# A four-layer adapter block on one core: another order of work inside the slots of its attention stage

## The reference

```python
x = x + einsum('bsi,boi->bso', x, w0[ids])                     # a whole 512x512 weight per sequence
x = x + attention(x)                                           # 32 query heads, 8 key/value heads, D = 128
x = x + einsum('bnr,bor->bno', einsum('bni,bri->bnr', x, B[ids]), A[ids])      # rank 16
x = x + x @ W.T + b + 2 * ((x @ lora_A[slot]) @ lora_B[slot])                  # rank 16
```

```python
def lora_linear(x, w, a, b, ids):
    return x @ w + einsum('btr,bro->bto', einsum('bti,bir->btr', x, a[ids]), b[ids])
p = softmax(where(causal & mask, q @ k.T / sqrt(D), -max))
out = lora_linear(p @ v, wo, ao, bo, ids)
```

## Time and profile before

| | |
|---|---|
| time, median of 3 runs | 808.75 us (807.19 to 808.94) |
| profiled execution | 807.25 us, its span 805.6 us |
| granted TensorE clock, mean | 0.972 of full |
| busy share of the span | PE 93%, PEld 77%, DVE 67%, ACT 40%, POOL 38% |
| attention stage | TensorE from 203.98 us to about 740 us |

### The profile page before, as it was taken

The page is one execution under the profiler, slowest core; times in us unless marked ns, Lnnn a source line. Parts: engine busy times, 40 slices in busy tenths (PEclk is TensorE's granted clock), DMA queues, the critical chain, the costliest instruction groups (busy, mean ns, idle before and its releaser), DMA issues. The chain is left out here.

```text
span 805.6 us, 13257 instructions
## 1 busy us (share of the span) xinstructions
PE 748.7 (93%) x4132; PEld 622.4 (77%) x4132; DVE 537.8 (67%) x1412; ACT 321.5 (40%) x908; POOL 307.5 (38%) x276
## 2 busy tenths in 40 slices
PE   5799398996799999999999999999999999987898
PEld 4688276885688888888888888888888888875686
DVE  4795366886566776667676677666767666653973
ACT  3663233210543453454354345435435433442540
POOL 3554410444362272273345237227324522510410
PEclk9999789999799999999999999999999999999899
DMA  8977777763042124035024112403402212611402
GB/s 296 307 242 212 253 202 213 268 181 113 1 126 58 46 86 118 1 94 153 0 65 131 52 56 74 117 0 109 139 0 65 65 39 66 106 16 33 102 27 79
DMA packets 75228, 86.84 MB, mean 108 GB/s; under 512 B 26791, under 2 KB 44359, under 8 KB 73975
## 3 DMA queue, kind: packets, MB, share of 16 engines
q1 hardware_dynamic: 73138, 79.83, 34.2%
q0 software_dynamic: 1760, 6.49, 2.6%
q10 hardware_dynamic: 292, 0.07, 0.0%
HBM read 71.40 MB, written 20.73 MB: 114 GB/s over the span
## 5 line engine op out<-in xcount | busy, mean ns | idle before, releaser
L994 POOL TENSOR_TENSOR prob<-prob,rinv 128x512 f32<-128x512 f32 x64 | 66.7, 1042 | 216.7 <-DVE rinv L1080 216.7
L943 ACT ACTIVATE prob<-sm,nmax 128x128 f32<-128x128 f32 x256 | 99.7, 391 | 77.9 <-DVE nmax L1065 77.9
L987 POOL TENSOR_TENSOR qt<-qc,qs 128x512 f32<-128x512 f32 x60 | 77.7, 1295 | 95.3 <-DVE qs L1023 95.3
L1155 PE MATMUL ps_out<-wo_hi,ot_hi 128*128 128x512 f32 x256 | 106.6, 416 | 4.3 <-DVE ot_lo L1042 2.4
L932 ACT ACTIVATE ot_hi<-ps_o 128x512 fp32r<-128x512 f32 x64 | 38.1, 595 | 162.6 <-PE ps_o L1143 162.6
L80 PE MATMUL ps_q<-x1t_hi,blk_hi 128*128 128x512 f32 x240 | 100.8, 420 | 0.0
L1157 PE MATMUL ps_out<-wo_hi,ot_lo 128*128 128x512 f32 x256 | 100.6, 393 | 0.0
L1156 PE MATMUL ps_out<-wo_lo,ot_hi 128*128 128x512 f32 x256 | 99.6, 389 | 0.0
L82 PE MATMUL ps_q<-x1t_hi,blk_lo 128*128 128x512 f32 x240 | 95.9, 400 | 0.0
L81 PE MATMUL ps_q<-x1t_lo,blk_hi 128*128 128x512 f32 x240 | 95.8, 399 | 0.0
L1023 DVE TENSOR_TENSOR qs<-ps_q,sin_t 64x512 f32<-64x512 f32 x120 | 82.7, 689 | 3.7
(11 more groups left out here) (208 smaller groups left out, 1727.4 us busy)
## 6 DMA issues: line engine op xcount, KB each, us to landing
wo_raw<-in_wo SPq DMA_DIRECT2D x8, 1024.0 KB, 5.4
raw_w<-in_wq SPq DMA_DIRECT2D x8, 1024.0 KB, 6.8
w_raw<-in_w SPq DMA_DIRECT2D x7, 1024.0 KB, 6.7
raw_b<-bq_sel SPq DMA_DIRECT2D x56, 128.0 KB, 4.3
raw_b<-bkv_sel SPq DMA_DIRECT2D x16, 256.0 KB, 6.7
v_hi_d<-v_hi SPq DMA_DIRECT2D x16, 256.0 KB, 3.1
v_lo_d<-v_lo SPq DMA_DIRECT2D x16, 256.0 KB, 4.0
k_rot<-kr SPq DMA_DIRECT2D x16, 256.0 KB, 3.2
```

The costliest lines, as they stand in the source:

```text
L943: e = act.activation(prob[i][:, h, :], sm[:, h, :], ACT.Exp, bias=nmax[i][:, h:h + 1], scale=-1.0, accum_out=rsum[i][:, h:h + 1])
L987: pool.tensor_tensor(qt[:, half, h, :], qc[:, :], qs[:, :], ALU.add).then_inc(q_done, 1)
L994: pool.tensor_tensor(prob[i][:, :, :], prob[i][:, :, :], rinv[i][:, :].unsqueeze(2).broadcast_to([P, G, T]), ALU.mult).then_inc(prob_done, 1)
L1155: pe.matmul(ps_out[:, :], ot_hi[:, q], wo_hi[:, h, :], start=(h == 0), stop=False)
```

## The change

It reorders every engine's instructions in a slot of the attention stage; no arithmetic is added or removed.

- TensorE: `scores(t)`, `turn(t-1)`, `adapters(t-2)`, `outputs(t-2)`, `values(t-1)`, `queries(t+1)`. The adapter products are a function of their own, ahead of `outputs`, with a semaphore `ao_ready`. `queries` are made one slot ahead; `queries(0)` stands ahead of the first scores.
- VectorE: rotation of `t`, maxima of `t`, `pt(t-1)`, reciprocal, `add(t-2)` (was `t-3`), `ot(t-1)` (was `t-2`), then in slot 1 both parts of `wo`, in even slots `bq`. The special order for the last head's second half goes.
- ScalarE: `pt(t-1)` first, `ao` high in slot 1, exponentials, `wo` part 0 in slot 1, `ot(t-1)`, the other parts of `wo`, `bq`, `wq`.
- GpSimd: rotation first, `ao` low in slot 1, the product, `wo` parts 2 and 3 in slot 1, `wq`.

```diff
@@ scalar
                     def slots(g, first, last):
                         for b in range(B):
                             t = B * g + b
-                            number = t if first else None
+                            number = t - 1 if first else None
+                            if not first or b >= 1:
+                                pt(t - 1, number)
+                            if b == 1:
+                                if not first:
+                                    act.wait_ge(ao_ready, B * g)
+                                ao_hi_part(g)
                             act.wait_ge(max_done, t + 1)
...
                             e.then_inc(exp_done, 1)
+                            if b == 1:
+                                act.wait_ge(wo_in, 16 * (g + 1))
+                                if not first:
+                                    act.wait_ge(out_ready, B * g)
+                                wo_hi_part(g, 0)
                             if not first or b >= 1:
-                                pt(t - 1, None if not first else t - 1)
-                            if b < HALF and not last:
-                                act.wait_ge(q_ready, B * g + b + 1)
-                                wq_hi_part(g + 1, b)
+                                ot(t - 1, number)
+                            if b == 1:
+                                wo_hi_part(g, 2)
+                                wo_hi_part(g, 1)
+                                wo_hi_part(g, 3)
...
+                            if b < HALF and not last:
+                                act.wait_ge(q_ready, B * g + b + 1)
+                                wq_hi_part(g + 1, b)
@@ gpsimd
+                            if not (last and b >= HALF):
+                                rotate(t, (b // HALF + 1) % 2, b % HALF)
+                            if b == 1:
+                                pool.wait_ge(ao_hi_done, g + 1)
...
                             pool.wait_ge(inv_done, t + 1)
...
-                            if not (last and b >= HALF):
-                                rotate(t, (b // HALF + 1) % 2, b % HALF)
-                            if not last and b < HALF:
-                                wq_lo_part(G * g + b + 1, b)
                             if b == 1:
                                 for h in range(G // 2, G):
...
+                            if not last and b < HALF:
+                                wq_lo_part(G * g + b + 1, b)
@@ vector
                         dve.wait_ge(out_ready, t + 1)
                         dve.tensor_tensor(res[:, b, :], ps_out[:, :], res[:, b, :], ALU.add).then_inc(res_done, 1)
+                        dve.wait_ge(ao_ready, t + 1)
...
-                            early = last and b >= HALF
-                            if early:
-                                ot(t - 2)
+                            if not (last and b >= HALF):
+                                rotate(t, (b // HALF + 1) % 2, i)
                             dve.wait_ge(s_ready, t + 1)
...
                             m.then_inc(max_done, 1)
...
+                            if not first or b >= 1:
+                                pt(t - 1)
                             dve.wait_ge(exp_done, t + 1)
...
                             dve.reciprocal(rinv[i][:, :], rsum[i][:, :]).then_inc(inv_done, 1)
...
+                            if not first or b >= 2:
+                                add(t - 2, (b - 2) % B)
+                            if not first or b >= 1:
+                                ot(t - 1)
                             if b == 1:
                                 wo_lo_part(g, 0)
-                            if early:
-                                add(t - 2, b - 2)
+                                wo_lo_part(g, 1)
+                            if not last and b % 2 == 0:
+                                bq_lo_part(PAIRS * g + b // 2 + 1, b // 2)
@@ tensor
+                        mm.then_inc(out_ready, 1)
+
+                    def adapters(t, g, b):
+                        pe.wait_ge(ot_lo_done, t + 1)
                         if b == 0:
                             pe.wait_ge(ao_lo_done, g + 1)
                         pe.wait_ge(axo_done, t + 1)
...
-                        mm.then_inc(out_ready, 1)
+                        mm.then_inc(ao_ready, 1)
...
+                            if first and b == 0:
+                                queries(0, 1, 0)
                             scores(t, g, b)
-                            if b < HALF:
-                                queries(t, 1, b, None if first else (G * g, PAIRS * g))
-                            elif not last:
-                                queries(t, 0, b - HALF, (G * g + b - HALF + 1, PAIRS * g + 2))
                             if not first or b >= 1:
                                 turn(t - 1, (b - 1) % B)
                             if not first or b >= 2:
+                                adapters(t - 2, g - 1 if b < 2 else g, (b - 2) % B)
                                 outputs(t - 2, g - 1 if b < 2 else g, (b - 2) % B)
                             if not first or b >= 1:
                                 values(t - 1, g - 1 if b < 1 else g, (b - 1) % B)
 
+                            if b + 1 < HALF:
+                                queries(t + 1, 1, b + 1, None if first else (G * g, PAIRS * g))
+                            elif b + 1 < B and not last:
+                                queries(t + 1, 0, b + 1 - HALF, (G * g + b + 1 - HALF + 1, PAIRS * g + 2))
+                            elif not last:
+                                queries(t + 1, 1, 0, (G * (g + 1), PAIRS * (g + 1)))
```

## The result

| | before | after |
|---|---|---|
| time, median of 15 runs each | 807.39 us (802.71 to 811.52) | 816.22 us (812.39 to 819.54) |
| ratio, 95% interval | | 1.0106 (1.0084 to 1.0129) |
| span of the profiled execution | 805.6 us | 811.8 us |
| TensorE busy, share of the span | 748.7 us, 93% | 746.6 us, 92% |

The change makes the kernel slower by 1.1%, 8.8 us between the medians. The forecast was 810.3 us (+1.5, range 805.5 to 819), with VectorE as the winner of a race between two engines; 817.9 stood beside it for the case that GpSimd wins. GpSimd won.

The account below looks back on a forecast made before the run. TensorE, one gapless stream in the middle of the attention stage, was taken as the bound; 0 (middle slots) + 4.2 (start) + 0.6 (slot 1) - 3.3 (end) = +1.5 us on 808.75: 810.3 us, range 805.5 to 819.

Parts of the forecast that it names:

- a race between two engines: Slot 1 of a head: VectorE's and GpSimd's wo splits start within 0.05 us; 0.09 or 1.17 a head by winner.
- slower: Side of the whole time against the kernel before: slower 0.60, same 0.23, faster 0.17.
- rival 1: Slot 1 of a head: GpSimd wins in every head, 8.2 instead of 0.6, +9.1 us, 817.9 us; chance 0.32.
- Rival 3: Stage start isn't lost (bq_lo not blocked, clock holds) and slot 1 makes no wait: 806 us; chance 0.11.
- I take VectorE first, since the offset here is the smaller: Slot 1 of a head: VectorE's wo split beats GpSimd's, costing 0.09 a head, 0.6 us over 7 heads.
- the row at 422.90: Trace before: VectorE began 0.05 to 0.09 behind the second GpSimd split, ran its 0.67 undisturbed; cited against rival 1.
- the row at 173.30: Trace before: GpSimd split begun at 173.30; VectorE's, at 173.38, took 1.77 instead of 0.69; cited for rival 1.
- Middle slots: Gapless TensorE slots in mid-stage: same matmuls, same loss, 8.36 us each, change 0, bounds -0.05 and +0.05 a slot.
- 0.89 + 0.23 = 1.12: TensorE in a slot: scores plus one wide matmul, so the step from narrow to wide behind scores is free.
- Start: Start of the attention stage: VectorE's order makes TensorE pause, half clock follows; +4.2 us, ends 2.8 and 5.6.
- End: Last slots of the stage: 30.7 with queries ahead against 33.95 us, gain 3.3, bounds 2.3 and 4.
- Slack for pt_lo: Ordinary slot: VectorE's pt_lo reaches TensorE at s+4.22, 0.4 us before the values matmuls at s+4.63.

Follow-up runs that it names:

- e1: Changed kernel, but in slot 1 of each head ScalarE makes wo_hi 1 before 2, so GpSimd's first split starts behind VectorE's: 807.24 us, ratio 0.9984.
- e8: Changed kernel plus one useless 128x1 multiply on GpSimd in each head, ahead of its first wo split: 808.38 us, ratio 0.9992.
- e2: Changed kernel, but GpSimd begins its two wo splits only when both of VectorE's are done: 807.54 us, ratio 0.9991.
- e5: e2 with the adapters behind the outputs again: 810.4 us in one run.
- e6: e2 with the queries, still a slot ahead, between scores and transposes: 824.34 us in one run.
- e7: e2's wait plus e4's reordered start, with bq_lo(0) on VectorE in the gap before rotation 0: 801.81 us, ratio 0.9937 to the kernel before.
- e3: Changed kernel, but in the first head bq_lo part 0 stands at the end of VectorE's slot 1 instead of slot 0: 814.75 us, ratio 1.0088.
- e4: Changed kernel, start reordered: scores(0) before queries(0), maxima 0 before rotation 0, product 0 before sum 0, pt_lo(0) before slot 1's maxima, e3's bq_lo: 815.82 us, ratio 1.0090.

## Why the prediction was right and where it failed

- **The time** fell in the range and on the side forecast as likeliest (slower), but by the chain of rival 1, which had 0.32, and not by the forecast's: +8.8 us between the medians against a forecast of +1.5. That 817.9 is so near to 816.22 is in part luck: in the profiled executions rival 1's terms add up to 6.2 and not to 9.1, because the middle slots gained 2.2 and the start cost 1 less. (Rival 3's 806 is 805.5 by its own terms, 808.75 - 3.3; nothing hangs on it.)
- **The step that failed** is "I take VectorE first, since the offset here is the smaller". The race was seen and both outcomes were priced rightly: 0.09 and 1.17 a head forecast, 0.10 (e1, e8) and 1.19 (after) measured. The choice rested on the row at 422.90, where VectorE began behind GpSimd and ran undisturbed. Heads 1 to 6 of the kernel before all show that (VectorE 0.06 to 0.09 behind, 0.67 each). Against it stood the row at 173.30, where GpSimd came out of idle and VectorE, 0.08 behind, was blocked; here too GpSimd is idle (0.27) before its split, and in all eight heads of the changed kernel it went first with a lead of only 0.04. So the row from idle was the nearer one. What decides is not known. My reading was that GpSimd's instruction at 422.90 stood back to back with the one before, and that its recorded start is then too early. In e8, too, GpSimd's split was recorded from 428.34 while the instruction before it ran until 428.39. But another place in the trace of before speaks against that as the whole cause:

```profile
39.84 2.52 POOL L647 TENSOR_TENSOR blk_b<-raw_b,blk_b 64x512 fp32r<-64x512 f32 x2
...
41.18 2.33 DVE L484 TENSOR_TENSOR wt_lo<-w_raw,wt_hi 128x512 fp32r<-128x512 f32 x2
```

GpSimd's second instruction starts at 41.10, back to back with its first, VectorE's split 0.08 later, as at 422.90, and yet VectorE is blocked: its first takes 1.73. In the changed kernel, at 16.10, a VectorE split 0.02 behind a GpSimd one that came out of idle was not blocked (0.68), and GpSimd's took 1.83. Recorded starts less than 0.1 apart don't tell the winner in these traces.
- Beside it stood the rule of the Trainium skill ("SBUF — State Buffer", "SBUF: two separate sides"): an exclusive lock, held to the end by whichever starts first. The runs agree with it: e1, e2 and e8 changed only who is first or whether the two meet, and took the loss of 1.19 us a head away or down to 0.10. By recorded starts alone, 422.90 and 16.10 do not agree.
- **Middle slots**: forecast 8.36, bounds 0.05 to either side; measured 8.32, a gain of 2.2 us. The sum 0.89 + 0.23 = 1.12 was right, but rows with two decimals can't tell 0.02 from nothing, and 56 slots make a microsecond of it. This term was put at 0 and is the second one that was off; what gives the 0.04 is open, as e5 and e6 leave it.
- **Start**: forecast +4.2; 3.2 in the profiled execution and some 5 in e1's and e2's. The mechanism was as forecast: bq_lo blocked (1.32), pauses of 1.49 and 3.82 (forecast 1.7 and 4), half clock for 4.7 us (forecast 3.8).
- **End**: forecast -3.3, measured -3.3; slots of 5.28, 5.64, 5.58 and 5.56 for 5.32, 5.62, 5.57 and 5.57.
- **Slack for pt_lo**: forecast 0.4. In e1 and e8 VectorE's rotation of slot 2 begins 0.5 late and 0.10 reaches TensorE, so it is 0.4.
- **What came of the gain**: 2.2 + 3.3 are there in every version that keeps the change's order of TensorE behind the start (e5 and e6 don't). The race took 8.5 and the start 3 to 5. e7 removes both and keeps the rest.

## What to carry to other kernels

When a new order makes VectorE and GpSimd each start an instruction that reads two SBUF tensors, within a tenth of a microsecond of each other, don't forecast the winner from offsets of recorded starts: price both outcomes, or write the order down with a wait. A fix at the start of a stage has to be followed through two slots, since an engine that is late gives the delay back further down (e3, e4); it pays only when the work that it runs into is free of conflicts. An engine without gaps gains from a new order only what neighbours cost each other, and that has to be measured over many slots, not from two rows.

## What the runs showed that was not expected

- Where VectorE and GpSimd both had two splits to do, they took turns, instruction by instruction. VectorE's split of 0.67 us waited for a GpSimd split of 1.3 each time: 1.80 and 1.75 in the changed kernel.
- A tiny instruction on GpSimd (128x1, 0.19 us) moved the next one's start by 0.14 us, and with it 1.09 us a head.
- A gapless slot took 8.36, 8.34 and 8.32 us with three, two and one steps from narrow to wide matmuls. Whether the steps are the cause is open.
- Of two starts less than 0.1 us apart in the profile the later one was sometimes the one that went first (422.90 in the kernel before, 16.10 in the changed one).
- The stage begins at half clock, and its first queries group took 4.4 us in some executions and 5.6 in others, with the same order of work there. What decides between them these traces don't show.
